# A one-core layer kernel: the last group's chain by halves, its store by tiles, and two set-up steps moved between engines

## The reference

```python
x = x + attn_a(layernorm(x))      # linear attention: q, k = elu(.)+1; kv = k^T v per sequence; q kv / norm; Wo, bo
x = x + ffn(layernorm(x))         # squared relu(x Ws1) Ws2, plus experts with truncated weights (0 unless one weight is 1)
x = x + attn_b(layernorm(x))      # only the first 16 tokens of each sequence attend, three iterations; elsewhere it adds ob
x = x + ffn(layernorm(x))         # the same ffn once more
```

## Time and profile before

| | us |
|---|---|
| median of 3 runs (400.58 to 401.0) | 400.91 |
| the profiled execution: time | 400.6 |
| the profiled execution: span of its trace | 398.7 |
| PE busy | 373.1 (94%) |
| DVE busy | 297.6 (75%) |
| POOL busy | 249.7 (63%) |
| ACT busy | 234.2 (59%) |

### The profile page before, as it was taken

The page is one execution under the profiler, slowest core; times in us unless marked ns, Lnnn a source line. Parts: engine busy times, 40 slices in busy tenths (PEclk is TensorE's granted clock), DMA queues, the critical chain, the costliest instruction groups (busy, mean ns, idle before and its releaser), DMA issues.

```text
span 398.7 us, 7260 instructions
## 1 busy us (share of the span) xinstructions
PE 373.1 (94%) x2458; PEld 306.7 (77%) x2458; DVE 297.6 (75%) x677; ACT 234.2 (59%) x402; POOL 249.7 (63%) x305
## 2 busy tenths in 40 slices
PE   8879999999999999988879999999999998989993
PEld 4778989998999899876758887687667766677762
DVE  5688786778677866785696559887787879885574
ACT  3587776777677767544444755356454554364451
POOL 3388885788578855579373536787465845955302
PEclk9999999999999999999998999999999999999998
DMA  8831111111100000032530321233223321331103
GB/s 258 249 102 53 54 53 54 54 53 54 55 0 2 0 2 0 19 92 93 163 98 23 109 76 65 88 109 110 57 70 99 111 80 36 108 110 57 48 10 113
DMA packets 29625, 29.79 MB, mean 75 GB/s; under 512 B 5750, under 2 KB 25468, under 8 KB 29564
## 3 DMA queue, kind: packets, MB, share of 16 engines
q1 hardware_dynamic: 29004, 28.51, 23.3%
q10 hardware_dynamic: 560, 0.52, 0.5%
HBM read 19.98 MB, written 8.98 MB: 73 GB/s over the span
## 4 chain that ended last, share of the span: by engine, by line
PE 63%; DVE 18%; issue 7%; POOL 7%; ACT 3%; DMA 1%; DVEq 0%; POOLq 0%; ACTq 0%; SPq 0%
PE PB L1585 6%; DVE ln_bn L1109 5%; PE PA L1655 3%; PE PG L1436 3%; PE PA L1661 3%; PE PA L1656 3%; PE PG L1431 3%; PE PG L1432 3%; PE PT L1345 2%; PE PT L1632 2%; DVE x_all L1163 2%; DVE x_all L1171 2%; POOL o_lo L535 2%; PE PB L1390 2%; PE PA L1390 2%
## 5 line engine op out<-in xcount | busy, mean ns | idle before, releaser
L535 POOL TENSOR_TENSOR o_lo<-q_all,o_hi 128x512 fp32r<-128x512 f32 x32 | 40.2, 1279 | 33.5 <-ACT o_hi L811 33.5
L518 POOL TENSOR_TENSOR xn_pair<-scratch,xn_pair 128x512 fp32r<-128x512 f32 x32 | 41.9, 1308 | 30.6 <-ACT xn_pair L654 30.6
L1585 PE MATMUL PB<-ws,scratch 128*128 128x256 f32 x240 | 58.8, 388 | 1.6 <-DVE x_all L1171 1.5
L1585 PEld LDWEIGHTS PB<-ws,scratch 128*128 128x128 f32 x240 | 44.2, 192 | 15.4 <-issue 10.6
L1109 DVE BATCH_NORM_STATS2 ln_bn<-x_all 128x6 f32<-128x256 f32 x128 | 44.9, 413 | 0.9
L511 POOL TENSOR_TENSOR x_all<-x_all,wvo 128x1024 f32<-128x1024 f32 x16 | 45.3, 2833 | 0.0
L527 POOL TENSOR_TENSOR q_all<-q_all,scratch 128x512 f32<-128x512 f32 x32 | 41.3, 1313 | 0.0
L818 ACT ACTIVATE scratch<-PB,ln_rsq 128x256 f32<-128x256 f32 x28 | 11.7, 470 | 41.1 <-issue 25.9
L935 DVE TENSOR_TENSOR o_lo<-scratch,o_hi 128x512 fp32r<-128x512 f32 x32 | 32.8, 1024 | 4.1 <-ACT o_hi L672 2.7
L1431 PE MATMUL PG<-xn_pair,o_hi 128*128 128x256 f32 x128 | 32.1, 285 | 2.0 <-ACT o_hi L672 2.0
L647 ACT ACTIVATE scratch<-x_all,ln_shift,ln_rstd 128x255 f32<-128x255 f32 x60 | 31.0, 596 | 4.0 <-POOL ln_shift L507 4.0
(11 more groups left out here) (283 smaller groups left out, 1101.3 us busy)
## 6 DMA issues: line engine op xcount, KB each, us to landing
scratch<-inv_scratch SPq DMA_DIRECT2D x32, 256.0 KB
x_all<-n_L_attn_a_inputs_q_dram SPq DMA_DIRECT2D x15, 512.0 KB, 3.5
out_dram<-x_all SPq DMA_DIRECT2D x15, 512.0 KB, 5.7
inv_scratch<-inv_turned SPq DMA_DIRECT2D x16, 32.0 KB
out_dram<-x_all SPq DMA_DIRECT2D x2, 256.0 KB, 2.3
x_all<-n_L_attn_a_inputs_q_dram ACTq DMA_DIRECT2D x2, 128.0 KB, 2.8
x_all<-n_L_attn_a_inputs_q_dram SPq DMA_DIRECT2D x2, 128.0 KB, 2.9
setup<-in_L_attn_a_Wq_dram ACTq DMA_DIRECT2D x1, 256.0 KB, 4.9
```

The source lines that it names most:

```text
L518: nc.gpsimd.tensor_tensor(halves[:, :, 1, :], pair(xn[n % 2], h), halves[:, :, 0, :].bitcast(F32), ALU.subtract).then_inc(x_lo, 1)
L535: nc.gpsimd.tensor_tensor(o_lo[:, c, :], q[:, c, :], o_hi[:, c, :].bitcast(F32), ALU.subtract).then_inc(o_lo_done, 1)
L1585: last = mm(four(dst)[:, t, :], h[:, t * P:(t + 1) * P], ws2[:, :], start=(t % 2 == 0 and not onto_rows), stop=True, skip_group_check=True)
```

## The change

Six things change; what is computed stays the same.

1. **Opening.** DVE takes `stats(1)` ahead of the split of the q half of the weights, and normalises tiles 0 and 1 of the second group itself; ACT has tiles 2 and 3 only. Who reads the group waits for both.
2. **bo of the last group.** `add_bo(15)` leaves the end of pass 1 and goes to step 1, slot 3, on POOL.
3. **Special tokens.** The three block weights (L1228) go to POOL, in step 1, slot 1, with a semaphore of their own for the three loads they need. On DVE the centering matrix goes to slot 2 of step 2 (behind L1153), the selector and the maxima to slot 2 of step 3, the small row to slot 2 of step 4.
4. **`row_scales(1)`** stands ahead of the products of step 1, as in all other steps.
5. **Step 16.** Variances come in two parts, of the group r as soon as its statistics are there, then of v, with a reciprocal each; ACT lays ob into PB before the relu, not behind it; the third product of the last group goes behind the down product; DVE takes the last statistics by halves, each behind its half of L1171.
6. **Step 17 and the stores.** The last variances are DVE's own (five small instructions and a reciprocal); the last down product signals by pairs of tiles, and DVE adds each pair when it is there; the last group is stored tile by tile, tiles 0 and 2 by SP, 1 and 3 by ACT. The special rows wait only for the stores of the first four groups.

The diff, cut to its core:

```diff
@@ SP @@
-                        sp.dma_start(dst, w.rearrange("(o r) e -> o r e", o=1).to_broadcast([HC, HD, HD])).then_inc(c_vecs, 16)
+                        sp.dma_start(dst, w.rearrange("(o r) e -> o r e", o=1).to_broadcast([HC, HD, HD])).then_inc(c_rows, 16)
...
                 if v == NG - 1:
-                    for h in range(2):
-                        sp.wait_ge(out_dve, dve_tiles(v) + 2 * h + 2)
...
+                    for t in range(0, T, 2):
+                        sp.wait_ge(out_dve, dve_tiles(v) + t + 1)
+                        sp.dma_start(out_dram[nv, :, t:t + 1, :], x_tile(nv, t)).then_inc(stored, 16)
...
-            sp.wait_ge(stored, 16 * (NG - 1))
+            sp.wait_ge(special_rows_stored, 16 * B)
@@ POOL @@
             x_low(0, 0)
+            pool.wait_ge(norm1_dve, T - 1 + T // 2)
             rstd(2)
...
-                add_bo(n)
+                if n < NG - 1:
+                    add_bo(n)
...
+                if i == NG:
+                    pool.wait_ge(bn2, T * NG)
+                    variances(5 * (i - 1), slice(0, 1))
+                    pool.wait_ge(bn3, T * (v + 1))
+                    variances(5 * i, slice(1, 2))
...
-                if (i, slot) == (0, 3):
+                if (i, slot) == (1, 1):
+                    pool.wait_ge(c_rows, 16 * 3)
+                    for rows16, blk in zip(l_rows, l_blk):
+                        nc.gpsimd.tensor_tensor(blk.rearrange("p (h e) -> p h e", e=HD),
...
+                elif (i, slot) == (1, 3):
+                    add_bo(NG - 1)
@@ ACT @@
-                for t in range(T):
+                for t in range(0 if n > 1 else T // 2, T):
...
+                if i == NG:
+                    lay_ob(i, r, v)
                 if runs(r):
                     act.wait_ge(f1_mm, r + 1)
...
+                if i == NG + 1:
+                    for t in range(1, T, 2):
+                        act.wait_ge(out_dve, dve_tiles(v) + t + 1)
+                        act.dma_start(out_dram[nv, :, t:t + 1, :], x_tile(nv, t)).then_inc(stored, 16)
@@ DVE @@
             weight_lo(slice(0, D), PA[:, :, 0:D], 0)
             xt_low(0)
+            stats(1)
             weight_lo(slice(D, 2 * D), PG[:, :, 0:D], 1)
...
-            stats(1)
+            normalise_tiles(1, range(T // 2))
...
+            def last_variances():
...
+                dve.wait_ge(rsq, NG + 1)
+                dve.wait_ge(bn3, T * NG)
...
+                nc.vector.reciprocal(ln_rsq[:, 1, :], a).then_inc(rsq, 1)
...
                 for t in range(by_dve(v)):
+                    dve.wait_ge(f4_mm, v + 1 + (t // 2 if v == NG - 1 else 0))
...
+                        if i == NG:
+                            dve.wait_ge(f2_added, 2 * r + h + 1)
+                            dve.wait_ge(var, 5 * (i + 1))
+                            x_stats(nr, 1, bn3, (2 * h, 2 * h + 1))
...
-                if at == (2, 1):
...
+                if at == (2, 2):
...
+                elif at == (3, 2):
...
+                elif at == (4, 2):
@@ PE @@
-                if runs(r) and i != 1:
+                if runs(r):
                     row_scales(i)
...
-                if i == 1:
-                    row_scales(i)
-                if runs(r):
+                if runs(r) and i < NG:
                     pe.wait_ge(f1_scaled, r + 1)
...
+                    third_product(r)
...
                     down(PB, h2s, f2_mm, True)
+                    if i == NG:
+                        third_product(r)
```

More of the change, by code:

```diff
@@ L612, in step @@
                     scale_query(i + 1)
-                if runs(r) or runs(v):
+                if runs(r):
                     ge(pool, rsq, i - 1)
-                    variances(i, r, v)
+                    step_variances(i, r, v)
                 if 1 <= i < B:
@@ L907, in first_ln1, with normalise_tiles @@
                     nc.vector.bn_aggr(ln_mv[:, 0, t:t + 1, :], ln_bn[:, 0, t:t + 1, :]).then_inc(stat1, 1)
-            def first_normalise():
-                dve.wait_ge(pow1, 2)
-                for t in range(T - 1):
-                    nc.vector.tensor_scalar(xn[0][:, t:t + 1, 0:D - 1], x_tile(0, t)[:, :, 0:D - 1], ln_mv[:, 0, t, 0:1],
+            def normalise_tiles(n, tiles):
+                dve.wait_ge(pow1, 3 * n + 2)
+                for t in tiles:
+                    nc.vector.tensor_scalar(xn[n][:, t:t + 1, 0:D - 1], x_tile(n, t)[:, :, 0:D - 1], ln_mv[:, 0, t, 0:1],
                                             ln_rstd[:, 0, t:t + 1], ALU.subtract, ALU.mult).then_inc(norm1_dve, 1)
@@ L1165, in step @@
                     ge(dve, var, 5 * i)
-                    x_stats(n, 0, bn2)
+                    x_stats(n, 0, bn2, range(T))
                 if runs(r):
@@ L1175, in step @@
                     dve.wait_ge(f2_added, 2 * r + 2)
-                    ge(dve, var, 5 * i)
-                    x_stats(nr, 1, bn3)
+                    if i < NG:
+                        ge(dve, var, 5 * i)
+                        x_stats(nr, 1, bn3, range(T))
                     run_experts(r, nr)
@@ L1580, in fold_ffn_product, with down @@
                 last.then_inc(fold_mm, 1)
-            def down(dst, h, done, onto_rows):
+            def down(dst, h, done, onto_rows, by_pair=False):
                 for t in range(T):
@@ L1586, in down @@
                               skip_group_check=True)
-                    if onto_rows and t % 2 == 1 or t == T - 1:
+                    if t == T - 1 or (onto_rows or by_pair) and t % 2 == 1:
                         last.then_inc(done, 1)
@@ L1596, in row_scales, with third_product @@
                 last.then_inc(r2_mm, 1)
+            def third_product(r):
+                mm(PT[:, 0, :], wc, h2s, start=False, stop=True, skip_group_check=True).then_inc(f3_mm, 1)
             def step(g, b):
@@ L1623, in step @@
                         pe.wait_ge(f2_added, 2 * (v + 1))
-                    down(f4_pair(v), h3, f4_mm, False)
+                    down(f4_pair(v), h3, f4_mm, False, v == NG - 1)
                 chain(i, 1)
```

112 lines of the change are left out of this document (67 added, 45 removed).

## The result

| | before | after |
|---|---|---|
| median, us (range) | 400.75 (399.08 to 401.0) | 389.51 (389.47 to 390.02) |
| profiled execution: time; span | 400.6; 398.7 | 389.48; 387.6 |

The ratio is 0.9743 (95% interval 0.9705 to 0.9782); by the medians the kernel is 11.2 us faster.

A forecast was written before the change was run, and what follows sets the result against it. Mostly PE's own queue sets the time (63% of the chain), with gains where the chain leaves PE. 1.6 + 0.7 + 1.8 + 2.8 + 1.7 + 2.4 = 11.0 off 400.6 gives 389.6; predicted 389.8, range 387.3 to 394.5.

The forecast's parts named there:

- 1 opening: Opening: earlier statistics and shared normalising start the first exponentials near 16.8; 1.6 us off, bounds 0.9 to 1.95.
- 2 end of pass 1: End of pass 1: without POOL's `add_bo(15)` beside it the last `k_low` shortens and PE's wait goes; 0.7 us, 0.57 to 1.1.
- 3 step 1: Kernel's step 1: with `row_scales(1)` early, DVE's L1163 starts as soon as PE's products end; 1.8 us off.
- 4 step 2: Kernel's step 2: special-token work moved off DVE removes PE's 2.82 idle before the third product; 2.8 us, from 2.0.
- 5 clock: Behind step 2's gap: PE's granted clock of 0.57 over 208 to 212 returns to full; 1.7 us, 0 to 1.7.
- 6 tail: Steps 16 and 17 and last stores: last additions 2.3 earlier, stores 0.1; 2.4 us off, 1.5 to 3.4.
- the discount: Opening: one more `k_low` may meet `x_low`, up to 1.1 us back; 1.6 taken within 0.9 to 1.95.
- the covers: Waits meant to hide moved work: POOL's 2.91 idle in the kernel's step 1; DVE's 1.1 a step before L1163.
- A: Kernel's step 2: token copy or POOL's later variances hold PE and the clock still falls; 392.9 us, chance 0.16.
- C: Kernel's step 1: POOL's block weights far dearer, delaying PE and lowering its clock; slower, 405 us, chance 0.04.
- B: Opening and end of pass 1 give nothing, as POOL's chain paces the early turns; 392.1 us, chance 0.08.
- D: Tail gives less: last variances and down product come in turn; 390.7 us, chance 0.66 together with the forecast.

The follow-up runs named there:

- 5: The kernel after with `add_bo(15)` back at the end of pass 1; 390.3 us against 389.51.
- 7: The kernel after with SP's three block-weight row loads behind its inverse-norm rows' load and `add_bo(15)` back at the end of pass 1; 389.96 us.
- 1: The kernel before with the change's opening alone; 397.91 us against 400.21.
- the four kernels above: The kernel after (389.51 us) and three variants: last store as two SP halves (390.2), as four SP tiles (390.02), third product ahead in step 16 (390.63).
- 8: The kernel after with the last group's store as before, two halves both issued by SP; 390.2 us.
- 9: The kernel after with the last group's four tile stores all issued by SP; 390.02 us.
- number 4: The kernel before with 20 unused products more on PE in the gap of step 2, nothing moved; 399.21 us against 400.21.
- number 12: The kernel before with two small memsets and their waits more at the start of DVE's program; 400.08 us against 400.13.
- kernel 3: The kernel before with the changes to steps 16 and 17 and the stores alone; 397.78 us against 400.21.
- Number 6: The kernel after with SP's three loads of the block weights' rows moved behind its load of the inverse-norm rows; 388.75 us.

## Why the prediction held, and where it didn't

389.8 was forecast, 389.51 came. The sum is nearer than its terms are:

| term | predicted | measured after | from |
|---|---|---|---|
| 1 opening | 1.6 | 1.45 | 5: 1.45, 7: 1.49, 1: 1.43 net |
| 2 end of pass 1 | 0.7 | 0.02 | (1.83 - 0.36) - 1.45 |
| 3 step 1 | 1.8 | 1.71 | 3.54 - 1.83 |
| 4 step 2 | 2.8 | 2.97 | 6.51 - 3.54 |
| 5 clock | 1.7 | 1.63 | 8.14 - 6.51 |
| 6 tail | 2.4 | 2.08 | (10.54 - 8.96) + 0.50 |
| not priced | 0 | 1.18 | 0.36 + 0.82 |

The six terms give 9.86 and not 11.0; 1.18 of what no step priced fills the hole. A hit to 0.3 us is thus in part luck: without the head start and the drift of steps 3 to 15 it would have been about 390.7, still inside the range.

**Step 2, end of pass 1, failed.** "PE waited 0.57 for it ahead of L1436 ... so the wait goes": it went, and the last product of pass 1 came 0.94 earlier (2.75 - 0.36 - 1.45). What failed is the sentence ahead of the steps, "Nothing there waits for a moment fixed from outside, so I take it that a gain made early is still there at the end." I followed it on PE; the next thing late was on SP's queue, where the inverse-norm rows' load stands behind three other loads. The change's own SP lines leave them there. In before POOL did not wait for that load, so no row pointed at it, and I did not read its queue. Over the four kernels above 0.02 to 0.59 is left of it.

**Step 6 was mis-sized, in two places that offset.** Up to the last L1128 1.58 came and not 2.3. I put the third product's end at 389.6 and the first pair at 391.9. (The variances on DVE, put at 391.95, came at 383.13 + 8.96 = 392.09.) On before's time (plus 8.96) ACT started its pair at 389.99, and the pair released DVE at 392.63. The first came 0.39 late. 0.1 of it is a slip in my sum (384.7 + 0.65 + 1.73 is 387.1, not 387.0; 378.14 + 8.96 = 387.1 came). For the rest I took the chain's pieces, 1.74 and 0.86, which end where the next PE instruction starts, for the time at which a result is there. The profile's own durations (1.99, 1.02) end later: from the down product's start to ACT's start it is 381.03 - 378.14 = 2.89, not 2.60. The second lost another 0.34 the same way: four products to a release take 383.67 - 382.43 = 1.24, not 0.9. Some 0.3 of handover for each crossing from PE was missing. The Trainium skill, Perfetto Trace Analysis, Tensor Engine Instruction (MATMUL, LD_WEIGHTS), says that PE's shown end is an estimate and the semaphore comes behind it; here ACT began 0.04 behind the shown end (380.99), so the shown end was the right one to take, and the chain's piece was not. The stores gave 0.50 where I had 0.1; 0.3 of it is shown by numbers 8 and 9.

**Steps 1, 3, 4 and 5 held**, and but for one discount for their reasons. In step 1 the exponentials start behind PE's last product, 16.48 + 0.36 = 16.84 on before's time (predicted 16.8). But they started at 18.64 before, not at 18.74, so the upper bound was 1.8 and not 1.95; and the discount was meant for a long `k_low`, while 0.25 of the 1.70 net at half-turn 30 was lost behind ACT's later start in the last half-turn. For the others: the first addition of step 1 gains 1.71; PE does not stand in step 2; number 4 shows the clock apart, on the trace. Of the covers, POOL's gap held (1.12 in what was 2.91), the variances behind `add_bo(15)` cost nothing, and the copy was late (1.05) without holding PE. Rivals A and C did not come, and of B only the half on the end of pass 1, by a load and not by POOL's chain; D (390.7) named the right place, the tail, for the wrong reason.

**What stays open.** Of the 0.82 in steps 3 to 15, 0.46 is step 9's, which number 12 ties to the place in DVE's program. The rest, 0.36, has no cause that I can show; kernel 3, which changes nothing there either, moved by 0.46 from step 3 to step 15. Why kernels whose programs are the same there keep such different shares of part 2 (1.47 to 2.04 net at the reciprocal) was not tried. No run undid `row_scales(1)` alone, so that step 1's 1.71 is its doing rests on the traces. (All upper bounds of the prediction add up to 12.75, not 12.9; nothing hangs on it.)

**A faster version.** Number 6 ran in 388.75 (388.43 to 389.04), below every execution of the kernel after; on the traces it wins 0.94 net at step 1 over the profiled execution of after, and 0.37 (2.41 - 2.04) over number 8, which kept most. The intervals of the two ratios overlap, so in times alone the gain isn't settled.

## What to carry to other kernels

Follow a gain past the engine that makes it: ask which DMA the next step needs, and what its queue issues ahead of it; here three small loads ate up to 0.9 us until they were moved behind. For a handover from PE take the profile's durations to the consumer's start, not the pieces of the chain, which end where PE goes on. And check a sum that came out right by its terms: shifts of single events between two traces show which term paid.

## What the runs showed of the hardware that was not expected

- 20 products more in a wait of PE made the kernel faster: the granted clock stayed at 1.00 (2.4 GHz) over 208 to 212 and not 0.57, worth 1.63 us net on the traces and 1.0 us between the medians.
- A delay of 0.49 of one DVE instruction, with only DVE's own last one to wait for, went with two memsets 290 us earlier, and ACT started one instruction 0.3 later behind the same product of PE. The page of after counts 31 packets on each of two instruction queues; the Trainium skill, Runtime: NRT & Kernel Launch, Instruction fetch mechanics, has each engine fetch its program in blocks by a DMA, mostly hidden. Whether these delays are such fetches no run here shows.
- The first k and q product, which stands behind the first loads, started up to 1.1 us apart in the 14 profiled executions (11.39 to 12.52), and at the end of pass 1 that difference was still there (1.02 and 0.99 between number 8 and the kernel after).
